# The listed counts of the second batch scaled by TensorE into a PSUM bank before VectorE adds them to the weights

## The reference

```
x = x + causal_attention(prior_attention(x, prior mask, listed keys, u))
x = x + mixture_of_experts(mixer(x))
```

```
use_sparse = lam >= 1
dense:  softmax(scores - lam * not(prior_mask))
sparse: softmax over the 32 listed keys of each query
```

## Time and profile before

| | us |
|---|---|
| median of 3 runs | 1714.3 (1708.88 to 1715.85) |
| the profiled execution | 1709.51 |
| its span in the trace | 1707.8 |
| mean granted TensorE clock, share of full speed | 0.947 |
| PE busy | 1576.6 (92%) |
| DVE busy | 924.8 (54%) |
| ACT busy | 726.6 (43%) |
| POOL busy | 692.2 (41%) |

### The profile page before, as it was taken

One profiled execution on the slowest core, in us unless ns is written; L12 is line 12 of the kernel. 1 busy time (PEld: TensorE's weight loads), 2 busy tenths in 40 slices (PEclk: granted clock), 3 DMA queues, 4 the chain that ended last, 5 costly groups with the idle time before them and its releaser, 6 DMA issues. The chain is left out here.

```text
span 1707.8 us, 20452 instructions
## 1 busy us (share of the span) xinstructions
PE 1576.6 (92%) x7376; PEld 765.0 (45%) x7376; DVE 924.8 (54%) x2079; ACT 726.6 (43%) x990; POOL 692.2 (41%) x483
## 2 busy tenths in 40 slices
PE   5889989878998998999989988999999999999998
PEld 3423323222332332433343323545666567777755
DVE  7678878789867876646766463325232111111141
ACT  4854656455465565557655557133221111111110
POOL 5437989776789899434221102220000300000070
PEclk8569999998999999999998989999999999999999
DMA  3560122231313212223632012300040003424061
GB/s 99 149 155 20 44 54 60 69 86 47 93 44 77 55 33 50 60 77 99 163 90 56 8 51 87 122 18 0 1 148 1 25 0 125 144 99 170 16 121 27
DMA packets 75906, 121.43 MB, mean 71 GB/s; under 512 B 14921, under 2 KB 53266, under 8 KB 72732
## 3 DMA queue, kind: packets, MB, share of 16 engines
q1 hardware_dynamic: 72155, 113.62, 23.6%
q0 software_dynamic: 3072, 6.03, 2.1%
q10 hardware_dynamic: 576, 0.47, 0.1%
HBM read 85.08 MB, written 36.96 MB: 71 GB/s over the span
## 5 line engine op out<-in xcount | busy, mean ns | idle before, releaser
L1131 POOL TENSOR_TENSOR sb_prob<-sb_prob,sb_weight 128x1024 f32<-128x1024 f32 x192 | 450.6, 2369 | 80.0 <-ACT sb_prob L1339 79.3
L1339 ACT ACTIVATE sb_prob<-wide 128x1024 f32<-128x1024 f32 (+3 forms) x384 | 347.6, 917 | 252.1 <-PE wide L1960 149.9
L1955 PE MATMUL wide<-sb_stack_q,sb_stack_k 99*128 99x512 bf16 (+3 forms) x896 | 285.7, 367 | 21.3 <-DVE sb_prob L1679 8.7
L1626 DVE CUSTOM_DVE_ANT_0 sb_junk<-bank,sb_bias 128x512 bf16<-128x512 f32 x348 | 231.5, 686 | 55.9 <-PE bank L1928 53.4
L1383 ACT ACTIVATE sb_sil<-wide 128x320 f32<-128x320 f32 (+1 forms) x128 | 66.2, 517 | 436.0 <-PE wide L2034 436.0
L1928 PE MATMUL bank<-sb_stack_k,sb_stack_q 96*128 96x512 bf16 (+3 forms) x604 | 220.1, 382 | 31.7 <-DVE sb_rowmax L1626 16.3
L2034 PE MATMUL wide<-sb_weight,sb_ffn 128*128 128x512 f32 x512 | 232.9, 598 | 0.0
L1975 PE MATMUL wide<-sb_prob,sb_v_aug 128*17 128x512 f32 (+3 forms) x1792 | 225.2, 572 | 7.1 <-ACT sb_o_raw L1352 6.8
L1771 DVE TENSOR_TENSOR sb_act_s<-sb_sil,wide 128x512 f32<-128x512 f32 x64 | 43.9, 686 | 252.8 <-ACT sb_sil L1383 252.8
L1620 DVE TENSOR_REDUCE sb_rowmax<-bank 128x1 f32<-128x512 f32 (+3 forms) x256 | 134.2, 548 | 64.2 <-PE bank L1931 49.2
L1136 POOL TENSOR_SCALAR_AFFINE_SELECT sb_prob<-sb_prob 128x256 f32<-128x256 f32 x128 | 51.4, 410 | 244.1 <-ACT sb_prob L1339 243.6
(11 more groups left out here) (265 smaller groups left out, 1881.3 us busy)
## 6 DMA issues: line engine op xcount, KB each, us to landing
sb_stack_k<-parts SPq DMA_DIRECT2D x32, 256.0 KB, 6.9
o_raw<-sb_o_raw SPq DMA_DIRECT2D x32, 256.0 KB, 2.3
sb_big<-rg SPq DMA_DIRECT2D x8, 1024.0 KB, 4.9
sb_big<-ru SPq DMA_DIRECT2D x8, 1024.0 KB, 7.2
sb_big<-rd SPq DMA_DIRECT2D x8, 1024.0 KB, 10.7
sb_stack_q<-parts SPq DMA_DIRECT2D x16, 384.0 KB, 5.0
parts<-sb_o_norm SPq DMA_DIRECT2D x40, 128.0 KB
sb_stack_q<-parts SPq DMA_DIRECT2D x16, 256.0 KB, 5.4
```

The costliest lines, as they stand in the source:

```text
L1131: e.tensor_tensor(p, p, weight_of(*u[1:]), ALU.mult).then_inc(weigh_p.handle, 1)
L1339: e.activation(p[:, :, first:HALF], sc[:, :, first:HALF], ACT.Exp).then_inc(SC.empty_sem(u), 1)
L1626: e.tensor_tensor_reduce(out=junk[:, i % 2, 0:hi - lo], in0=BK.tile(u)[:, 0:hi - lo], in1=bias[:, qt, lo:hi], scale=1.0, scalar=-3e38, op0 ...
L1955: i = e.matmul(sc[:, j * HALF + first:(j + 1) * HALF], stack_k[0:ROWS_M, n % 3, g, kt * P:(kt + 1) * P], stack_q[0:ROWS_M, n % 3, g, half ...
```

## The change

The product flag x counts moves from VectorE to TensorE. A new constant `keep` is the identity times the sparse flag of batch 1 (128x128, bf16), made once by VectorE at the start. For each of the 16 pieces of batch 1 TensorE multiplies `keep` with the counts into a bank, as one more user of the three banks (`"listed"` is added to `BANKED`), and VectorE adds that bank to `weight` with a plain `tensor_tensor`, which also frees the bank. The signal `weight_d` goes; who waited for it waits for the bank to be emptied. TensorE, not VectorE, now waits for the load of the counts. Batch 0 is made as before. In the diff the first `"listed"` branch is VectorE's, the second TensorE's.

```
-BANKED = ("product", "v", "max", "turn", "y", "resid")
+BANKED = ("product", "v", "max", "turn", "y", "resid", "listed")
...
-late += [(i, ("kw_load", 1, kt, half)), (i + 3, ("kw", 1, kt, half)), (i + 4, ("kw_sum", 1, kt, half))]
+late += [(i, ("kw_load", 1, kt, half)), (i + 3, ("kw", 1, kt, half)), (i + 4, ("listed", 1, kt, half))]
...
+        keep = s1("keep", [P, P], BF16)
...
-            return weight_d.after((b, kt, half)) if b else weight_p.after((b, kt, half, "sum"))
+            return BK.emptied(("listed", b, kt, half)) if b else weight_p.after((b, kt, half, "sum"))
...
+            e.tensor_scalar(keep[:], C["ident"], fl[3][:, 1:2], None, ALU.mult).then_inc(cut_d.handle, 1)
...
-                elif kind == "kw_sum" and u[1]:
-                    _, b, t, half = u
-                    o = weight[:, t, half * HALF:(half + 1) * HALF]
+                elif kind == "listed":
+                    o = weight[:, u[2], u[3] * HALF:(u[3] + 1) * HALF]
                     w.wait_ge(tables_a.after(("kw", *u[1:])))
-                    w.wait_ge(listed_in[t % 2].after(u[1:]))
-                    e.scalar_tensor_tensor(out=o, in0=listed_w[t % 2],
-                                           scalar=fl[3][:, b:b + 1], in1=o, op0=ALU.mult,
-                                           op1=ALU.add).then_inc(weight_d.handle, 1)
+                    w.wait_ge(BK.filled(u))
+                    e.tensor_tensor(o, BK.tile(u)[:], o, ALU.add).then_inc(BK.empty_sem(u), 1)
...
+                elif kind == "listed":
+                    w.wait_ge(listed_in[u[2] % 2].after(u[1:]))
+                    w.wait_ge(cut_d.after("keep"))
+                    w.wait_ge(BK.vacant(u))
+                    e.matmul(BK.tile(u)[:], keep[:], listed_w[u[2] % 2], start=True, stop=True).then_inc(BK.full_sem(u), 1)
```

More of the change, by code:

```diff
@@ L762, in build @@
         bias_d = signal("dve_bias", [u[1:] for u in of("kb")])
-        weight_p = signal("pool_weight", [(*u[1:], z) for u in of("kw_sum") if u[1] == 0 for z in ("sum",)])
+        weight_p = signal("pool_weight", [(*u[1:], z) for u in of("kw_sum") for z in ("sum",)])
         listed_a = signal("act_listed", [u[1:] for u in of("kw") if u[1] == 0])
         unlisted_a = signal("act_unlisted", [u[1:] for u in of("kw") if u[1] == 0])
-        cut_d = signal("dve_cut", range(B))
+        cut_d = signal("dve_cut", [*range(B), "keep"])
         capped_p = signal("pool_capped", [u[1:] for u in of("score") if on_diagonal(u[1], *place(*u[1:])[0:2])])
-        weight_d = signal("dve_weight", [u[1:] for u in of("kw_sum") if u[1]])
         split_p = signal("pool_split", of("second", "third"))
@@ L1115, in _ @@
                     e.tensor_tensor(lo, val, mid, ALU.subtract).then_inc(split_p.handle, 1)
-                elif u[0] == "kw_sum" and u[1] == 0:
+                elif u[0] == "kw_sum":
                     _, b, t, half = u
@@ L1360, in _ @@
                     else:
-                        w.wait_ge(weight_d.end)
+                        w.wait_ge(BK.emptied(of("listed")[-1]))
                     e.activation(y1[:, mc, half * HALF:(half + 1) * HALF], BK.tile(u)[:], ACT.Identity,
```

## The result

| | before | changed |
|---|---|---|
| median of 9 runs, us | 1708.88 (1704.13 to 1718.36) | 1698.06 (1693.87 to 1701.87) |
| span of the profiled execution, us | 1707.8 | 1696.3 |
| mean granted TensorE clock | 0.947 | 0.957 |

The ratio is 0.9926, 95% interval 0.9904 to 0.9948: 12.6 us faster, between 8.9 and 16.4; the two medians of the table differ by 10.8 us, which lies within that. The forecast was 10.5 us. The medians of three runs shown ahead of the prediction had put the kernel before 5.4 us higher than nine runs do.

What follows compares the result with a forecast made beforehand. VectorE was taken to bound the 80 us stretch; 12.2 us from the pace, less 1.5 for the denominators' wait and 0.2 for `keep`, gave 10.5 us, from 1714.3 to 1703.8 us, range 1695 to 1712.

Steps and rivals of the forecast that it cites:

- What bounds the stretch, and why: 361 to 441 us: VectorE, 94% busy, sets the pace; its adds with two SBUF tensors wait for GpSimd.
- The add: VectorE's 16 adds of counts: 24.4 us become 9.8, a relief of 14.6 us (ends 0.9 and 14.6).
- The matmul: 16 more matmuls on TensorE: free where VectorE is the bound, 3.5 us uncovered, 6.9 us at half clock.
- The pace: The 80 us from 361 to 441: VectorE's 60.6 us at 89.4% busy make 67.8 us, 12.2 us less.
- the like stretch: 151 to 202 us, same kinds of units without weights made: VectorE 89%, TensorE 96%, clock 1.00; used as reference.
- The first piece: TensorE at 358.98 us waits for the counts' load, landing at 361.1: cost 0 to 0.5 us, taken as 0.
- The end of the stretch: Before VectorE's reciprocal: a wait of 2.3 to 3.1 us for the denominators' loads, charged 1.5 us, bounds 0 and 3.1.
- A: Rival, chance 0.20: TensorE becomes the bound of the stretch at clock 0.89; gain 5 us, 1709 us.
- B: Rival, chance 0.12: VectorE's relief is eaten by its next waits; gain 0 to 4 us, 1712 us.
- C: Rival, chance 0.06: TensorE waits for a load and a lent bank, clock falls to half; 15 us slower, 1729 us.

Runs made afterwards that it cites:

- the denominators first: On the changed kernel, the denominators' loads put ahead of the loads of the stacks at the start of every job: 1719.81 us, ratio 1.0057.
- the prior attention alone: On the changed kernel, remainders of the maxima moved to GpSimd and denominators' loads ahead of the stacks' in the prior attention only: 1687.76 us, ratio 0.9852.

## Why the prediction was right

*What bounds the stretch, and why.* Right, and now shown by runs. The long adds are waits of an instruction with two SBUF tensors for GpSimd's multiplies: the same add has a median of 690 ns with its operand in a bank and of 1856 with it in SBUF, 32 columns wait as long as 512, and the long adds end a fixed time after a multiply of GpSimd's does. The Trainium skill, SBUF — State Buffer, section Who interferes with whom, says that a VectorE instruction with two SBUF inputs contends with a GpSimd instruction that reads SBUF, while one with at most one SBUF input, outside the 2-port perf modes, does not. The traces agree: up to 2875 ns with both in SBUF, 679 to 692 with one in a bank.

*The add.* 14.6 us of relief forecast. The busy time of the adds fell by 25.7 - 11.0 = 14.7 us. The term was right to 0.1 us. One reading in it was not: 742 ns against 686 is a difference of the two forms of the instruction and says nothing of where the operand lies. The plain add took 679 ns at best with both tensors in SBUF too.

*The matmul.* Costed at nothing, with 3.5 us if uncovered. Doubling it lengthened neither the total nor the stretch, so it was covered, as far as these runs can tell.

*The pace.* 12.2 us forecast, from the rate of the like stretch, with 67.8 us left of 80. From first to last add it was 69.1, 10.1 us less than 79.2, so this term was too large by about 2 us, and 69.1 lies just beyond the 67 to 69 that I had named. VectorE got to 92.5% busy, better than the 89.4% I had taken, but its busy time fell by 75.2 - 63.9 = 11.3 us, not by 14.6. There are two reasons. I took the relief of all 16 adds off a window that ends at 441.0, where the last of them starts: within the windows the adds fell from 23.4 us to 10.3, by 13.1 only. And line 1652 (1651 before), another instruction with two SBUF tensors, took 0.20 us in this place before and 1.99 now; I had named such an exchange only as a rival. The clock there was 0.95, where I had taken the 1.00 of the like stretch; what that cost no run separates.

*The first piece.* TensorE waited 3.32 us for the load, where I had 2.1, and its matmuls behind it ran at half clock from 361.3 on (0.61 to 0.63 us each). I charged 0. The kernel before waited 2.50 us for ScalarE at this very place and then ran at half clock too (0.61 us at 365.72), so most of it was paid already: from store 5 to the first add it is now 13.2 us against 12.5. The charge was 0.6 us too small.

*The end of the stretch.* A wait of 2.3 to 3.1 us was forecast and 1.49 came, and 1.5 us was charged for it. But from the start of the last add to store 8 it took 32.9 us against 33.8 before, 0.9 us less and not 1.5 more: the last add itself is shorter by 1.7 us, which the term of the pace had already counted, and little was lost to the wait. Removing the wait gave a stretch 2.3 us shorter in one pair of traces (the denominators first) and 0.7 us longer in another (the prior attention alone), and nothing in the total. So the charge was too high, by 2.4 us as the marks have it.

*The sum.* 10.5 us forecast, 10.4 in the stretch by the marks, 12.6 by the ratio of the runs. By the marks it is made of 10.1 at the pace, -0.6 at the first piece and +0.9 at the end, where the forecast has 12.2, 0 and -1.5; `keep` took 0.16 us from its start to the next instruction's, for 0.2. So a gain that was 2.1 us too large and a charge that was 2.4 us too large nearly cancelled. The mechanism and the size of the relief were right by reasoning; that the sum came out to 0.1 us was luck. The forecast time, 1703.8 us, was 5.7 us above the measured 1698.06, and 5.4 of that is the median of before, which nine runs put lower than three.

*The rivals.* A, TensorE as the bound at the old clock, is spoken against by the clock of 0.95 and by the doubled matmuls, though five of them reach it. B, that the waiting moves, was true for 1.8 us at line 1652 and 1.5 us at line 1575. C, a lent bank that stops TensorE, has its price in the run with the add from SBUF: 9 us in the stretch if the add is long.

## What to carry to other kernels

When a VectorE instruction's duration varies several times over while its shape does not, look at where its operands lie before looking at its size. Here an instruction with two tensors in SBUF stood behind the GpSimd instructions beside it, for up to 7.3 us, and TensorE behind it. The wait is part of the duration, with no idle time shown before it; comparing its end with the ends of GpSimd's instructions finds it. Get one operand into PSUM, if TensorE has the time for it, or give a small instruction to GpSimd itself; shortening it takes off the work but not the wait. When subtracting a relief from a window, count only the instructions that lie in it. And charge a wait at what it stops: removing the 1.5 us for the denominators' load gained nothing in the total, while moving that load ahead everywhere cost 20 us elsewhere.

## What the runs showed of the hardware that was not expected

An instruction of VectorE can stand through several GpSimd instructions in a row, not only through the one that is running. None of the long adds stood for more than the length of one multiply, but line 1648 did. GpSimd's timeline of the changed kernel, beside the line 1648 shown above (start and duration in us; x2 are two instructions in one row):

```profile
531.97 4.73 POOL L1131 TENSOR_TENSOR sb_prob<-sb_prob,sb_weight 128x1024 f32<-128x1024 f32 x2
536.61 1.20 POOL L1115 TENSOR_TENSOR sb_tables<-sb_o_norm 128x512 bf16<-128x512 f32 x1
537.72 4.68 POOL L1131 TENSOR_TENSOR sb_prob<-sb_prob,sb_weight 128x1024 f32<-128x1024 f32 x2
```

Line 1648 started at 535.70, while the second multiply of the first row ran, and ended at 542.46, just after the last multiply did at 542.40. It stood through that one and the three behind it. What decides how many pass has not been tried.
